# Tables ahead of folded weights; the plain norm of x and the expert probabilities on ScalarE; one complex product on VectorE; GpSimd's scales in another order

## The reference, cut to what matters

```python
x  = x0 + block(plain_norm(x0))            # x0: 8 batches x 1024 tokens x 128
def block(x):                              # all in fp32
    h  = layernorm(x) * gamma + beta
    h  = real(ifft(fft(filter) * fft(h)) + last * prog * phazor)   # per channel, along the tokens
    x1 = h + x
    return silu(layernorm(x1) @ w1 + b1) @ w2 + b2 + x1
h = plain_norm(x)                          # then a mixture of experts on every token
logits = h @ router.T                      # 8 experts, the best 2
p = softmax(top2(logits))
out = x + sum_k p_k * (gelu(h @ mw1[e_k] + mb1[e_k]) @ mw2[e_k] + mb2[e_k])
```

## Time and profile before

| | us |
|---|---|
| median of 3 runs | 570.46 |
| fastest | 570.36 |
| the profiled execution | 572.02, of it the span 570.2 |

### The profile page before, as it was taken

How to read it: one execution, slowest core, us unless ns; L and a number is a source line. 1 busy time by engine, 2 the same in 40 slices (tenths; PEclk the granted TensorE clock), 3 DMA queues, 4 the chain that set the end, 5 groups by cost and what they waited for, 6 DMA issues and landing times.

```text
span 570.2 us, 11651 instructions
## 1 busy us (share of the span) xinstructions
PE 439.9 (77%) x2813; PEld 375.3 (66%) x2813; DVE 385.7 (68%) x1515; ACT 285.1 (50%) x602; POOL 311.2 (55%) x367
## 2 busy tenths in 40 slices
PE   1070359887797959788877895579999999999991
PEld 1030247675776758767675784568898988899881
DVE  7719969989788867972725773346666666666661
ACT  2740536678447376635525342345555555555540
POOL 6933686866688888585332564224434344433442
PEclk9995559999987979899978988899999999999996
DMA  8420000000111101011031345432222222222210
GB/s 260 142 89 0 1 0 2 1 0 2 40 40 41 39 30 51 21 60 68 31 98 31 99 156 172 162 98 81 76 73 78 83 84 79 85 81 80 61 32 0
DMA packets 33284, 37.44 MB, mean 66 GB/s; under 512 B 5254, under 2 KB 29331, under 8 KB 33092
## 3 DMA queue, kind: packets, MB, share of 16 engines
q1 hardware_dynamic: 27236, 23.56, 14.0%
q0 software_dynamic: 5984, 13.13, 6.7%
HBM read 19.52 MB, written 18.92 MB: 67 GB/s over the span
## 4 chain that ended last, share of the span: by engine, by line
PE 46%; DVE 15%; POOL 12%; issue 9%; ACT 4%; SPq 4%; DMA 0%; POOLq 0%; DVEq 0%; ACTq 0%
PE down_p L1011 14%; PE up_p L987 7%; PE up_p L988 6%; PE up_p L1003 6%; POOL sorted_rows L591 4%; DVE stats L1098 3%; PE down_p L839 3%; PE turn_p L811 2%; POOL work L582 2%; PE down_p L996 2%; ACT rows L694 2%; SPq L430 2%; PE route_p L872 1%; POOL scale L562 1%; SPq L431 1%
## 5 line engine op out<-in xcount | busy, mean ns | idle before, releaser
L630 POOL DMA_INDIRECT out<-result,out_id x91 | 91.0, 1000 | 147.0 <-DVE result L1480 135.8
L781 ACT ACTIVATE hid<-up_p 128x512 f32<-128x512 f32 x91 | 54.4, 598 | 112.4 <-PE up_p L988 112.4
L1011 PE MATMUL down_p<-mw_sb,hid_t 128*128 x728 | 101.9, 284 | 2.6 <-DVE result L1480 1.5
L1449 DVE TENSOR_SCALAR hid<-hid,tin 128x256 f32<-128x256 f32 x182 | 57.5, 358 | 59.0 <-ACT hid L781 58.4
L591 POOL DMA_INDIRECT sorted_rows<-rows,pos x64 | 72.8, 1137 | 42.6 <-issue 41.7
L1011 PEld LDWEIGHTS down_p<-mw_sb,hid_t 128*128 128x128 f32 x728 | 91.0, 196 | 6.7 <-issue 4.4
L839 PEld LDWEIGHTS down_p<-w_sb,work 128*128 128x128 f32 x512 | 63.4, 200 | 5.3 <-issue 4.9
L839 PE MATMUL down_p<-w_sb,work 128*128 128x128 f32 x512 | 66.3, 285 | 0.0
L660 ACT ACTIVATE work<-up_p,b_all 128x512 f32<-128x512 f32 x64 | 42.3, 683 | 44.2 <-PE up_p L825 44.1
L987 PE MATMUL up_p<-mw_c,xt 128*128 x182 | 58.8, 405 | 3.1 <-ACT xt L776 1.7
L811 PE MATMUL turn_p<-ident,work 128*128 128x128 f32 x192 | 30.3, 309 | 38.3 <-DVE work L1166 29.3
(11 more groups left out here) (244 smaller groups left out, 857.8 us busy)
## 6 DMA issues: line engine op xcount, KB each, us to landing
tin<-sorted_rows SPq DMA_DIRECT2D x91, 136.0 KB, 2.1
resid<-in_x SPq DMA_DIRECT2D x8, 512.0 KB, 3.7
sorted_rows<-zeros SPq DMA_DIRECT2D x29, 136.0 KB, 4.0
out<-result,out_id POOLq DMA_INDIRECT x91, 2.3
work<-in_mw SPq DMA_DIRECT2D x1, 1024.0 KB, 6.3
sorted_rows<-rows,pos POOLq DMA_INDIRECT x64, 2.5
work<-in_w SPq DMA_DIRECT2D x1, 256.0 KB
w_sb<-in_w SPq DMA_DIRECT2D x1, 256.0 KB
```

The lines of the kernel that those rows point to most:

```text
L630: g.indirect_dma_start(out_rows, bass.IndirectOffsetOnAxis(out_id[k][:, :], 0), result[k][:, :], None, bounds_check=TOKENS - 1, oob_is_err ...
L781: s_.activation(hid[s % 2][:, :], mid_p[s % 2][:, :], ACT.Gelu).then_inc(s_gelu, 1)
L1011: last = t.matmul(y_p, hid_t[s % 2][:, c * 128:(c + 1) * 128], mw2_sb[:, bass.ds(at, D)], start=c == 0, stop=c == 2 * EC - 1)
L1449: last = d.tensor_scalar(part, part, tin[s % INS][:, at:at + 1], None, ALU.mult)
```

## The change

- `bias_diagonals` (ScalarE's first half of `fold_weights`) stands ahead of iteration -3. The six copies (`folded_copies`) and TensorE's folding matmuls stand behind iteration -2. GpSimd's two table products stand right behind iteration -3, its `sort_constants` behind iteration -2. VectorE's `pair_facts` stands behind iteration 0. TensorE waits for the sort constants in `place(0)`.
- The plain norm xn is made from x by ScalarE, eight activations for each batch (`x0_plain_norm`, between `high` and `x0_norm`). `x0_unnorm` and `x0_unscale` are gone. GpSimd computes both scales and both shifts in `x0_scales`, in two buffers by batch.
- u * in_im goes from GpSimd (`u_product`) to VectorE, behind u * in_re.
- GpSimd's order in an iteration is `x1_scales`, `x2_scales`, `x0_scales`, four transfers, `v_product`, four transfers.
- The gap of the two logits gets its sign from VectorE ahead of the tanh, at the end of `choose`. ScalarE writes both probabilities by two more activations behind the tanh, ahead of `x2_norm`. The copy of the token number moves to `positions`.

```diff
@@ -142,9 +142,8 @@
         eps = sb("eps", [128, TPB])
         tmp = sb("tmp", [128, 8, TPB])
         var_eps = sb("var_eps", [128, 2, TPB])
-        norm_pow = sb("norm_pow", [128, 2, TPB])
-        shift0 = sb("shift0", [128, TPB])
-        unscale0 = sb("unscale0", [128, TPB, 1])
+        scale0 = [sb(f"scale0{q}", [128, 2, TPB]) for q in range(2)]
+        shift0 = [sb(f"shift0{q}", [128, 2, TPB]) for q in range(2)]
...
@@ -540,19 +537,15 @@
 
                 pool.wait_ge(s_x0m, b + 1)
                 after(pool, s_hn, b)
+                after(pool, s_xn, b - 1)
                 var = mom0[:, :, 1]
                 g.tensor_tensor(var_eps[:, 0, :], var, eps[:, :], ALU.add)
                 g.tensor_tensor(tmp[:, 2, :], mom0[:, :, 0], neg_one[:, :], ALU.mult)
                 then(g.tensor_scalar(var_eps[:, 1, :], var, 1.0 + EPS, EPS * EPS, ALU.mult, ALU.add))
-                then(g.tensor_tensor(norm_pow[:, :, :].rearrange("p a b -> p (a b)"),
+                then(g.tensor_tensor(scale0[b % 2][:, :, :].rearrange("p a b -> p (a b)"),
                                      var_eps[:, :, :].rearrange("p a b -> p (a b)"), neg_half[:, :], ALU.pow))
-                g.tensor_tensor(shift0[:, :], tmp[:, 2, :], norm_pow[:, 1, :], ALU.mult).then_inc(s_sc0, 1)
-
-            def x0_unscale(b):
-                pool.wait_ge(s_sc0, b + 1)
-                after(pool, s_xn, b)
-                then(g.tensor_tensor(tmp[:, 3, :], var_eps[:, 1, :], norm_pow[:, 1, :], ALU.mult))
-                g.tensor_tensor(unscale0[:, :, 0], tmp[:, 3, :], norm_pow[:, 0, :], ALU.mult).then_inc(s_un, 1)
+                g.tensor_tensor(shift0[b % 2][:, :, :], tmp[:, 2:3, :].to_broadcast([128, 2, TPB]), scale0[b % 2][:, :, :],
+                                ALU.mult).then_inc(s_sc0, 1)
...
-            def u_product(b):
+            def v_product(b):
+                pool.wait_ge(s_vi, b + 1)
                 if b == 0:
                     pool.wait_ge(s_tab, 1)
-                pool.wait_ge(s_u, b + 1)
-                after(pool, s_conv, b)
-                g.tensor_tensor(vi, u, in_im, ALU.mult).then_inc(s_ui, 1)
-
-            def v_product(b):
-                pool.wait_ge(s_vi, b + 1)
                 g.tensor_tensor(vi, vi, out_im, ALU.mult).then_inc(s_ti, 1)
...
                 b0, b1, b2, b3, chosen_b = i - 1, i + 1, i + 2, i + 3, i - 2
-                late = i == -1
-                if live(b3) and not late:
-                    x0_scales(b3)
                 if live(b1):
                     x1_scales(b1)
                 if live(b0):
                     x2_scales(b0)
-                if live(b2):
-                    u_product(b2)
-                    if late:
-                        x0_scales(b3)
+                if live(b3):
+                    x0_scales(b3)
                 if live(chosen_b):
                     sort_rows(chosen_b, range(0, 4))
                 if live(b2):
                     v_product(b2)
-                if live(b3):
-                    x0_unscale(b3)
                 if live(chosen_b):
                     sort_rows(chosen_b, range(4, TPB))
 
             decay()
             iteration(-3)
-            sort_constants()
             pool.wait_ge(s_low_high, 1)
             g.tensor_tensor(grid(out_im), slow[0], fast[1], ALU.mult)
             g.tensor_tensor(grid(in_im), slow[1], fast[0], ALU.mult).then_inc(s_oim, 1)
-            for i in range(-2, LAST + 1):
+            iteration(-2)
+            sort_constants()
+            for i in range(-1, LAST + 1):
                 iteration(i)
...
-                after(a, s_xn, b)
                 for j in range(TPB):
-                    last = s_.activation(hn[:, j, :], tile_of(resid, b, j), ACT.Identity, bias=shift0[:, j:j + 1],
-                                         scale=norm_pow[:, 1, j:j + 1])
+                    last = s_.activation(hn[:, j, :], tile_of(resid, b, j), ACT.Identity,
+                                         bias=shift0[b % 2][:, 1, j:j + 1], scale=scale0[b % 2][:, 1, j:j + 1])
                 last.then_inc(s_hn, 1)
+
+            def x0_plain_norm(b):
+                after(a, s_x1, b)
+                for j in range(TPB):
+                    last = s_.activation(xn[:, j, :], tile_of(resid, b, j), ACT.Identity,
+                                         bias=shift0[b % 2][:, 0, j:j + 1], scale=scale0[b % 2][:, 0, j:j + 1])
+                last.then_inc(s_xn, 1)
...
-            def tanh(b):
+            def probabilities(b):
+                q = rows[b % ROWBUFS]
                 a.wait_ge(s_gap, b + 1)
-                after(a, s_prob, b)
-                s_.activation(th[:, :, :], gap[:, :, :], ACT.Tanh, scale=0.5).then_inc(s_tanh, 1)
+                s_.activation(th[:, :, :], gap[:, :, :], ACT.Tanh).then_inc(s_tanh, 1)
+                a.wait_ge(s_tanh, b + 1)
+                s_.activation(q[:, :, R_PA:R_PA + 1], th[:, :, :], ACT.Identity, bias=half_pow[:, 0:1], scale=0.5)
+                s_.activation(q[:, :, R_PB:R_PB + 1], th[:, :, :], ACT.Identity, bias=half_pow[:, 0:1], scale=-0.5)\
+                    .then_inc(s_prob, 1)
...
                     silu_act(i, 3)
                 if live(b1):
                     high(b1)
+                if live(b2):
+                    x0_plain_norm(b2)
                 if live(b3):
                     x0_norm(b3)
 
-            def fold_weights():
...
+
+            def folded_copies():
+
                 for k in range(4):
                     a.wait_ge(s_fold, k + 1)
                     s_.activation(half(mw1_c, k), (up_p + [route_p])[k][:, :], ACT.Copy).then_inc(s_folded, 1)
...
+            bias_diagonals()
             iteration(-3)
-            fold_weights()
 
             a.wait_ge(s_ore, 1)
             s_.activation(in_re, out_re, ACT.Copy, scale=par[:, INIT_RE:INIT_RE + 1])
             s_.activation(vi, out_re, ACT.Copy, scale=par[:, INIT_IM:INIT_IM + 1]).then_inc(s_ire, 1)
-            for i in range(-2, 0):
-                iteration(i)
+            iteration(-2)
+            folded_copies()
+            iteration(-1)
...
+                if b == 0:
+                    pe.wait_ge(s_const, 1)
...
@@ -960,6 +960,7 @@
                 last = t.matmul(down_p[:, c:c + 1], w1_sb[:, c * 128:(c + 1) * 128], par[:, BETA:BETA + 1],
                                 start=True, stop=True)
             last.then_inc(s_b1raw, 1)
+            iteration(-2)
             pe.wait_ge(s_mw1, 16)
             pe.wait_ge(s_diag, 1)
...
-            for i in range(-2, 0):
-                iteration(i)
+            iteration(-1)
             pe.wait_ge(s_wsplit, 1)
             pe.wait_ge(s_b1, 1)
             pe.wait_ge(s_folded, 6)
-            pe.wait_ge(s_const, 1)
...
-            def x0_unnorm(b):
-                v.wait_ge(s_hn, b + 1)
-                v.wait_ge(s_un, b + 1)
-                d.tensor_tensor(xn, hn, unscale0[:, :, :].to_broadcast([128, TPB, D]), ALU.mult).then_inc(s_xn, 1)
-
             def rotate(b, between=None):
 
                 decay = decay_factor.to_broadcast([128, LENGTH])
                 v.wait_ge(s_u, b + 1)
+                after(v, s_conv, b)
                 rotated = mark(d.tensor_tensor(vr, u, in_re, ALU.mult))
+                d.tensor_tensor(vi, u, in_im, ALU.mult).then_inc(s_ui, 1)
...
-                after(v, s_tanh, b)
-                d.tensor_tensor(gap[:, :, :], best[:, :, :], runner[:, :, :], ALU.subtract).then_inc(s_gap, 1)
                 chain(d.tensor_tensor(scored[:, :, :], masked[:, :, :], wide(runner[:, :, :]), ALU.is_equal))
                 chain(d.tensor_tensor(scored[:, :, :], scored[:, :, :], wide(order[:, :, :]), ALU.mult))
                 chain(d.tensor_reduce(pick2[:, :, :], scored[:, :, :], AX, ALU.max))
+                d.tensor_tensor(best[:, :, :], best[:, :, :], runner[:, :, :], ALU.subtract)
                 d.tensor_tensor(first_low[:, :, :], pick1[:, :, :], pick2[:, :, :], ALU.is_gt)
                 chain(d.tensor_tensor(code[:, :, :], pick1[:, :, :], pick2[:, :, :], ALU.add))
+                after(v, s_tanh, b)
+                d.scalar_tensor_tensor(out=gap[:, :, :], in0=first_low[:, :, :], scalar=-0.5, in1=best[:, :, :],
+                                       op0=ALU.add, op1=ALU.mult).then_inc(s_gap, 1)
...
                 chain(d.tensor_tensor(placed[:, :, :], place_p, chosen[:, :, :], ALU.mult))
+                d.tensor_copy(rows[b % ROWBUFS][:, :, R_ID:R_ID + 1].bitcast(u32), batch_of2(token, b))
                 if live(b - 2):
                     v.wait_ge(s_sort[b - 2], 16 * TPB)
                 d.tensor_reduce(pos[b % 2][:, :].unsqueeze(2), placed[:, :, :], AX, ALU.add).then_inc(s_pos, 1)
-
-            def probabilities(b):
-
-                q = rows[b % ROWBUFS]
-                v.wait_ge(s_tanh, b + 1)
-                chain(d.scalar_tensor_tensor(out=signed[:, :, :], in0=first_low[:, :, :], scalar=-0.5, in1=th[:, :, :],
```

(25 more changed lines are left out.)

## The result

The median is 550.41 us (546.95 to 551.17), against 572.49 for the kernel before on the same chip: a ratio of 0.9614 with a 95% interval of 0.9556 to 0.9671. (The 572.49 is a median of four executions, one of which took 1122.68 us; the ratio leaves that one out.) Times 570.46 that is 548.4 us; 550.0 had been forecast. The profiled execution took 546.95 us, with a span of 545.2 us, against 572.02 and 570.2.

The account below looks back on a forecast made before the run. No engine fills an interval; the round of waits bounds the kernel. Terms -12.0 - 2.7 + 2.2 + 1.2 - 2.2 - 0.3 - 5.1 - 2.4 + 0.8 = -20.5 take 570.46 to 550.0 us, range 541 to 561.

Parts of the forecast that it names:

- The start: Up to the first x1_sum: -13.35 us from reordered lists and moved products, less 1.35 for late copies, gives 12.0.
- the folded copies: Start: six copies behind x0_norm(1) in ScalarE's list may delay the transposes, costing 0 to 2.7 us, taken as 1.35.
- the tables don't come first: Rival: in the start conv_turn(0) waits much longer for L971 and the copies, halving the gain; 562 to 570 us, chance 0.05.
- Iteration -1: Interval of 25.3 us: v_product at 16.9 after the sum without u_product ahead, pair_facts gone; 22.6, so -2.7 us.
- Iterations 0 and 1: VectorE's x_moments newly waits for GpSimd's x0_scales, now behind x1_scales and x2_scales: +2.2 and +1.2 us.
- Iterations 2 and 3: The choice covers the scales, scans start at 15.2, four transfers still hold v_product until 23.1: -2.2 and -0.3 us.
- Iterations 4 and 5: No statistics of x, TensorE not cold, in iteration 4 no wait for tanh: -5.1 and -2.4 us.
- The rest: The 322 us behind the eighth sum shift as a whole; added activations and later gap cost +0.8, from -0.3 to +2.
- The batch part gives nothing back: Rival: transfers keep v_product in place, scale waits cost iterations 2 and 3 too; start alone gains, 558 us, chance 0.24.
- More than forecast: Rival: table products overlap (3.7 us) and iterations 0 and 1 hide the scales (3.4): 537 to 545 us, chance 0.15.
- VectorE is held off by the powers: Rival: GpSimd's powers in the scales hold VectorE's two-input instructions to their end, costing 16 us; 566 us, chance 0.02.
- ScalarE's list is the bound: Rival: norms and next silu in one row, high late, put 26.6 us on the path in seven iterations; 582 us, chance 0.04.

Follow-up runs that it names:

- start_alone: The kernel before with only the start's new order of the lists: 578.03 us, ratio 0.9916 to the kernel before.
- without_start: The changed kernel with the old order of the start: 576.97 us, ratio 0.9897 to the kernel before.
- plain_norm_on_vector: The changed kernel with x0_unscale and x0_unnorm on VectorE as before, no x0_plain_norm: 565.42 us, ratio 0.9910 to the kernel before.
- u_on_gpsimd: The changed kernel with u * in_im back on GpSimd, behind x2_scales: 564.38 us, ratio 0.9883 to the kernel before.
- two_moment_buffers: The changed kernel with two buffers for x's moments, aggregation waiting for scales two batches back: 555.89 us (0.9566), on another chip 543.30 (0.9521).
- probabilities_on_vector: The changed kernel with tanh alone on ScalarE and the probabilities back on VectorE behind positions: 552.26 us, ratio 0.9660 to the kernel before.
- x0_scales_first: The changed kernel with x0_scales back ahead of x1_scales on GpSimd from iteration 0 on: 561.41 us, ratio 0.9644 to the kernel before.
- three ahead: The changed kernel with two buffers of moments and three transfers ahead of v_product instead of four: 542.75 us, ratio 0.9509 to the kernel before.

## Why the prediction was right

The forecast came out, and its mechanism in the main. To the eighth sum 21.3 us had been forecast and 22.7 came. That nearness is partly luck: the start gave 2.2 more than forecast and iteration 3 0.6 more, iteration 0 1.1 less.

**The start** was forecast at 12.0 and gave 14.2. The table products excluded each other as reckoned (2.93 us for L1376, done at 26.25, forecast 26.8); L1380 began at 28.42 (forecast 29.1); the wait of 11.95 us went. The term that was mis-sized is the folded copies: nothing, where 1.35 had been taken from between 0 and 2.7. The prediction had read the 2.05 us between L1166's end and the first sum as the transposes at the lower clock. They do take 1.97 there, but in both kernels VectorE's four operations of `weights` fill the same stretch. The first sum therefore came at 45.8 to 46.2 in all nine profiled executions with the whole of the start's gain (the changed kernel and all runs but start_alone, without_start, plain_norm_on_vector and u_on_gpsimd), while the transposes took 1.07 to 1.91 us. Of the other 0.8 us, 0.7 stand at L1380. The rival that the tables don't come first needed the copies to be late: start_alone, plain_norm_on_vector and u_on_gpsimd show it, at first sums of 53.9, 52.1 and 50.0. The prediction listed the plain norm's move under ScalarE's load, "hidden", and as VectorE's 1.2 us. That it is also what frees ScalarE's list in the start was not seen: the split of the forecast into "start" and "batches" was not a split by edits.

**Iteration -1:** -2.8 (forecast -2.7), with v_product at 16.7 us after the sum (forecast 16.9).

**Iterations 0 and 1:** +3.3 and +1.4 (forecast +2.2 and +1.2). The new wait of VectorE for GpSimd's scales was named, with its place; it is shown by its 3.90 and 4.06 us of idle time and by two_moment_buffers, which takes both away. In iteration 0 the term that failed is `pair_facts`, "behind iteration 0, where nothing waits for it", put at nothing. L1162 began 20.0 us after the sum, as the prediction's terms add up to, and 2.3 later than before. From there to the next sum it took 3.39 us instead of 2.42, for `pair_facts` stands between L1162 and x2_sum and x1_sum in VectorE's list. The gain of 1.1 us that the prediction counted in iteration -1 is paid back here. TensorE's clock looks like another cause: the transposes took 1.97 us at 89.63, behind 4.17 us of idle time. It cost nothing here, as two_moment_buffers shows. There the transposes ran at full clock (1.09 us at 85.93), and from L1162 at 84.65 to the sum at 88.04 it took the same 3.39 us:

```profile
84.65 1.23 DVE L1162 TENSOR_TENSOR work<-work 128x1024 f32<-128x1024 f32 x1 [0.60 <-POOL work L570]
...
86.91 1.20 DVE L1114 TENSOR_TENSOR rows<-down_p,resid 128x1024 f32<-128x1024 f32 x1
```

`pair_facts` at another place, with the rest of the change kept, wasn't run.

**Iterations 2 and 3:** -2.1 and -0.9 (forecast -2.2 and -0.3). By the timeline of iteration 2 the scans began 15.3 us after the sum (forecast 15.2), the transfers at 15.7 (15.9), v_product at 139.90, 23.3 (23.1), behind four transfers as in the earlier trace rows:

```profile
130.52 0.18 DVE L1103 BATCH_NORM_AGGREGATE mom<-stats 128x2 f32<-128x6 f32 x1 [0.21 <-POOL shift L547]
...
131.85 2.34 DVE L1154 TENSOR_TENSOR_SCAN work<-mag,start_v,work 128x1024 f32<-128x1024 f32 x1
...
132.24 3.01 POOL L579 DMA_INDIRECT sorted_rows<-rows,pos  x1 [1.85 <-DVE pos L1209]
...
139.90 2.36 POOL L570 TENSOR_TENSOR work<-work 128x1024 f32<-128x1024 f32 x1
```

The choice covers the scales, but only just: VectorE waited 0.21 us for them. The clock had been forecast low for both intervals, from the transposes of the start, which stood behind a wait of 18.63 us. It was low in iteration 2, where the transposes took 1.97 us at 143.57 behind a wait of 4.13. It was not in iteration 3, behind a wait of 4.03, and the 0.9 us that the transposes saved account for the 0.6 by which that interval beat the forecast:

```profile
172.75 1.09 PE L809 MATMUL turn_p<-ident,work 128*128 128x128 f32 x8 [4.03 <-DVE work L1162]
```

The length of the wait alone doesn't tell the two apart, and what does isn't shown.

**Iterations 4 and 5:** -5.0 and -2.4 (forecast -5.1 and -2.4). The scans began 12.9 us after the sum in both, 2.4 earlier than in iteration 2 (forecast 2.2), the transposes took 1.09 us, and VectorE no longer waited for tanh. That the order of the scales removed that wait is borne out by probabilities_on_vector, which keeps the new order and doesn't have it; x0_scales_first has its long wait for x1_scales in iteration 3 instead.

**ScalarE** has the 3.2 us a batch without harm. Behind x0_norm it stood idle until TensorE brought the next input of a silu: 3.81 us from iteration 0 to 1, 5.56 from 2 to 3, 4.38 from 3 to 4 (the row), but only 0.47 from 4 to 5. From 1 to 2 it had no idle time at all: the silu began at 117.17, right behind x0_norm, and TensorE's input had come at 117.13.

```profile
174.94 0.69 ACT L642 ACTIVATE work<-up_p,b_all 128x512 f32<-128x512 f32 x1 [4.38 <-PE up_p L823]
```

**The rest** was forecast at +0.8 and came at -2.3; as the executions scatter by more than that, neither is borne out.

**The rivals.** "The batch part gives nothing back" falls: without_start gives 7.3 us by itself, 6.2 of it behind the first sum. "More than forecast" asked for overlapping table products, which didn't come, and for hidden scales in iterations 0 and 1, which took the second buffer of moments: with it the kernel took 543.3 on one chip, inside that rival's 537 to 545, though with only one of its two terms. "VectorE is held off by the powers" falls by two more rows of the changed kernel, a power on GpSimd and a product of VectorE that began within it:

```profile
98.14 1.64 POOL L563 TENSOR_TENSOR scale<-tmp,neg_half 128x8 f32<-128x8 f32 x1
...
99.02 1.21 DVE L1149 TENSOR_TENSOR work<-work 128x1024 f32<-128x1024 f32 x1
```

Had the power held the product off until its end at 99.78, the row would be some 0.8 us longer. The Trainium skill, "SBUF — State Buffer", section "Who interferes with whom", says that the port pair which the two engines share is an exclusive lock, and that a VectorE instruction with two inputs in SBUF contends with a GpSimd instruction that reads SBUF. For the length of a power these rows disagree; for GpSimd's large products, as for the table products above, they agree (2.9 us each instead of 1.2 and 1.9). "ScalarE's list is the bound" didn't occur.

## What to carry to other kernels

When an operation moves to another engine, count not only its length in each batch (1.2 us of VectorE's) but who waited for it at its old place: ScalarE's norm had waited for that operation's buffer with the folded copies behind it, 5.1 us of the start. A change of order that makes a producer wait for its own buffer to be read (0.2 us in one iteration, 3.9 in another) is cured by a second buffer of 128x16 numbers, not by another order. And read the whole list of the engine that starts the next stage before a wait or a clock is blamed for when it starts: four small operations hid the folded copies and the clock in the start, and `pair_facts`, moved to where nothing was said to wait for it, took back in iteration 0 the 1.1 us that it had given in iteration -1.

## What had not been expected of the hardware

- GpSimd's small operations are held, too, by VectorE's large ones on SBUF. In the changed kernel L542, 0.20 us by itself, took 2.15 us at 53.88, beside a scan (53.71 to 56.04). The power L545 of 128x16, 2.90 us in the earlier trace rows, took 3.80 us at 58.49, where it began beside the product L1157 (58.34 to 59.54).
- An indirect transfer of GpSimd took 3.01 us when it began beside the first scan and 1.80 beside the second, 1 us before its end. It took 1.96 beside the subtraction L1162 (at 142.43), whose inputs are both in SBUF, and 0.96 beside x1_sum (at 145.97), which reads one of its inputs from PSUM. All others up to the eighth sum took 0.96 or 0.97, but for the like of these three in the later iterations (1.96 to 2.86). So the four ahead of v_product took 7.66 us in iteration 2, from 132.24 to 139.90, and one that is taken away from their end saves only the 1.27 us of a short one with its gap (1.3 in iteration 3 with three ahead).

```profile
53.88 2.15 POOL L542 TENSOR_TENSOR var_eps<-mom,eps 128x8 f32<-128x8 f32 x1 [0.58 <-DVE mom L1103]
...
58.49 3.80 POOL L545 TENSOR_TENSOR scale<-var_eps,neg_half 128x16 f32<-128x16 f32 x1
...
135.55 1.80 POOL L579 DMA_INDIRECT sorted_rows<-rows,pos  x1 [0.30 <-issue]
...
137.66 0.96 POOL L579 DMA_INDIRECT sorted_rows<-rows,pos  x1 [0.31 <-issue]
```

- The last part took 334 to 336 us on one chip and 319 to 327 on others, at equal intervals ahead of it; the one kernel that ran on both kinds, that with two buffers of moments, took 334.3 and 320.2. The cause stays open.
- TensorE's clock differed at equal waits: after waits of 4.13 and 4.03 us in one execution, and of 2.67 and 2.66 us in two, eight transposes took 1.97 and 1.09, and 1.89 and 1.09 us. The cause stays open.
